# Two tiles counted in a row before the applying products of both, in the first phase of layer 1

## The reference

```python
# layer 0 (gated, with edge types)
src_h = h[src] @ W_msg.T + b_msg
emb = edge_embed[jnp.clip(edge_type, 0, NUM_EDGE_TYPES)]
msg = src_h + emb
messages = jax.ops.segment_sum(msg, dst, num_segments=num_nodes)
h_new = _gru_cell(messages, h[:num_nodes], W_ih, W_hh, b_ih, b_hh)
x = layernorm(x + h_new)
# layer 1 (attention-like weights)
proj = feat @ fc_weight.T
w = sigmoid(e(proj[src], proj[dst]) * gate(proj[src], proj[dst]))
rst = (1 + eps) * feat + segment_sum(feat[src] * w, dst) / deg
x = layernorm(x + rst)
```

## Time and profile before

| what | value |
|---|---|
| median of 3 runs | 3123.31 us (3120.69 to 3128.86) |
| the profiled execution, own time | 3125.21 us |
| its span, first to last instruction | 3121.9 us |
| mean granted TensorE clock over the span | 0.774 |
| busy over the span | DVE 87%, PE 66%, POOL 65%, ACT 53% |

### The profile page before, as it was taken

One profiled execution on the slowest core, in us unless ns is written; L12 is line 12 of the kernel. 1 busy time (PEld: TensorE's weight loads), 2 busy tenths in 40 slices (PEclk: granted clock), 3 DMA queues, 4 the chain that ended last, 5 costly groups with the idle time before them and its releaser, 6 DMA issues. The chain is left out here.

```text
span 3121.9 us, 64562 instructions
## 1 busy us (share of the span) xinstructions
PE 2069.9 (66%) x14172; PEld 1774.5 (57%) x14172; DVE 2721.6 (87%) x13432; ACT 1639.6 (53%) x3644; POOL 2034.8 (65%) x2108
## 2 busy tenths in 40 slices
PE   5899999999873555555555555555555555555555
PEld 4588888888543454544545544554545545454455
DVE  3499899899477899999989999999999999999995
ACT  1287777777334444554445454555445444454543
POOL 1057677777203677777777777777777777777760
PEclk9999999999997666676666777667666676667665
DMA  4233333333206444444444444444444444444441
GB/s 104 64 86 98 94 98 97 96 95 98 79 24 199 129 133 142 134 140 134 134 140 133 140 134 137 137 137 137 133 142 133 140 134 133 142 133 140 133 136 42
DMA packets 251978, 375.77 MB, mean 120 GB/s; under 512 B 107569, under 2 KB 168922, under 8 KB 251834
## 3 DMA queue, kind: packets, MB, share of 16 engines
q0 software_dynamic: 99600, 272.13, 30.1%
q1 hardware_dynamic: 150022, 101.31, 11.8%
q10 hardware_dynamic: 2212, 0.60, 0.1%
HBM read 350.21 MB, written 23.65 MB: 120 GB/s over the span
## 5 line engine op out<-in xcount | busy, mean ns | idle before, releaser
L1511 POOL DMA_INDIRECT got<-rows,idx x1624 | 1551.0, 955 | 546.0 <-issue 500.7
L1712 PE MATMUL sum_ps<-whot,got 128*128 128x128 f32 x3264 | 697.6, 384 | 525.7 <-DVE whot L1523 426.1
L1712 PEld LDWEIGHTS sum_ps<-whot,got 128*128 128x128 f32 x3264 | 602.2, 276 | 604.1 <-DVE whot L1523 477.4
L1705 PE MATMUL er_ps<-win,hot_t 128*128 128x128 bf16 x4932 | 508.3, 278 | 399.8 <-ACT hot_t L1653 365.8
L1705 PEld LDWEIGHTS er_ps<-win,hot_t 128*128 128x128 bf16 x4932 | 453.4, 130 | 448.2 <-ACT hot_t L1653 401.3
L788 POOL DMA_INDIRECT got<-y_rows,idx x448 | 460.0, 1027 | 198.2 <-issue 133.9
L1523 DVE TENSOR_SCALAR whot<-iota_f,dl,w_s 128x128 f32<-128x128 f32 x1632 | 455.6, 359 | 144.6 <-ACT w_s L1658 144.5
L947 ACT CAST cols<-c_ps 128x318 fp32r<-128x318 f32 x1176 | 493.1, 440 | 145.3 <-PE c_ps L1033 107.3
L979 PE MATMUL span_ps<-y_parts,cols 128*126 128x256 f32 x2968 | 568.5, 319 | 0.2 <-ACT cols L947 0.2
L1649 ACT ACTIVATE apart<-dst_b,less 128x512 bf16<-128x512 int16 x406 | 290.0, 714 | 326.2 <-DMA dst_b<-dst_row 320.4
L979 PEld LDWEIGHTS span_ps<-y_parts,cols 128*126 128x126 f32 x2968 | 453.4, 192 | 5.3 <-issue 1.0
(11 more groups left out here) (248 smaller groups left out, 2023.7 us busy)
## 6 DMA issues: line engine op xcount, KB each, us to landing
dst_b<-dst_row SPq DMA_DIRECT2D x59, 512.0 KB, 4.1
got<-rows,idx POOLq DMA_INDIRECT x1624
dst_b<-dst_row SPq DMA_DIRECT2D x59, 384.0 KB, 4.0
win<-parts SPq DMA_DIRECT2D x118, 96.0 KB, 3.7
got<-y_rows,idx POOLq DMA_INDIRECT x448
parts<-split SPq DMA_DIRECT2D x13, 384.0 KB, 7.0
y_rows<-y_parts SPq DMA_DIRECT2D x1, 3332.0 KB
rows<-nodes SPq DMA_DIRECT2D x13, 256.0 KB, 2.5
```

Of the source, the lines that this page charges most:

```text
L1511: pool.indirect_dma_start(got[:, c, i, :], None, rows, bass.IndirectOffsetOnAxis(ap=idx1[:, c, i:i + 1], axis=0)).then_inc(gathered[c], 16)
L1705: mm = pe.matmul(er_ps[:, c, i * D:(i + 1) * D], hot_t[:, c, i * P:(i + 1) * P], win[:, int(c >= HALF), part, :], start=(part == 0), stop= ...
L1712: mm = pe.matmul(sum_ps[:, 0:P], got[:, c, i, D:2 * D], whot[:, c, i, :], start=(c == 0 and i == 0), stop=(c == NS - 1 and i == STEP - 1))
```

## The change

The counts are issued two at a time. At an even t the loop issues the counts of tiles t and t + 1, each with its own waits. At an odd t it issues none. What follows at each t (applying products, `ready`, `post`, the products of the bodies) stays where it was. Tile 20 is counted alone. Number and shape of all instructions stay the same, and no other engine's program changes.

```diff
                             for t in range(CG):
-                                n, s = 2 * CG * k + CG * h + t, (CG * h + t) % RING
-                                pe.wait_ge(made, n + 1)
-                                if not first or CG * h + t >= CB:
-                                    pe.wait_ge(c_copied, n - CB + 1)
-                                pe.matmul(c_ps[:, (CG * h + t) % CB, 0:HW], left[:, s, :], right[:, s, :],
-                                          start=True, stop=True).then_inc(counted, 1)
+                                n = 2 * CG * k + CG * h + t
+                                if t % 2 == 0:
+                                    for u in range(t, min(t + 2, CG)):
+                                        m, s = n - t + u, (CG * h + u) % RING
+                                        pe.wait_ge(made, m + 1)
+                                        if not first or CG * h + u >= CB:
+                                            pe.wait_ge(c_copied, m - CB + 1)
+                                        pe.matmul(c_ps[:, (CG * h + u) % CB, 0:HW], left[:, s, :], right[:, s, :],
+                                                  start=True, stop=True).then_inc(counted, 1)
                                 if t >= BLOCKS and not (first and h == 0):
                                     if t == BLOCKS:
                                         ready(g - 1)
```

## The result

| | before | changed |
|---|---|---|
| median | 3125.11 us (4 runs, 3120.69 to 3128.86) | 3147.61 us (4 runs, 3144.41 to 3148.80) |
| span of the profiled execution | 3121.9 us | 3142.6 us |
| first to last count (the touched stage) | 649.9 us | 669.7 us |
| mean granted clock over the span | 0.774 | 0.758 |

The ratio is 1.0069, 95% interval 1.0054 to 1.0085: the changed kernel is slower by 22 us. 3141 was forecast, with a range of 3128 to 3149. Of the 20.7 us between the two spans, 19.8 lie between the first and the last count.

A forecast was written before the change was run, and what follows sets the result against it. TensorE was taken to bound the touched stage. Group beginnings +18.5, written-out part +1.2 and pairs -2.2 made +17.5 us: 3142.7 from the profiled 3125.2, which lay 1.9 above the median, so 3141 expected, range 3128 to 3149.

The forecast's parts named there:

- TensorE sets the pace, and the loss reaches the end: Touched stage: TensorE busy 589 of 600 us, waiting 10.8 us for VectorE; its gain or loss reaches the stage's end.
- Where a group begins, 0.41 us at nine of ten: Loop groups' beginnings: two products (0.24 us) and `ready` (0.17) come behind the wait for tile 0's copy; 18.5 us in all.
- free kind: Group beginnings, one of ten, where the count of tile 3 doesn't wait for a copy, as at group 23: loss 0.
- The written-out part, 0.3 us each: Four groups in the written-out part wait in the same way at their beginning: 0.3 us each, 1.2 us in all.
- Gain inside a group, 0.01 us a pair, of which half was taken: Pairs (4, 5) to (18, 19), 440 in all: gain between 0 and 4.4 us, taken as 2.2 us.
- No wait inside a group: A pair's second count does not wait for the copy or matrices: zero added, with 0.04 to 0.23 us to spare.
- The granted clock stays 0.99: Touched stage: the granted clock was expected still at 0.99 in the changed kernel's profile.
- That the loss is only two products a start (no change): Rival for group beginnings: `ready` is issued ahead, pairs gain the full 0.01 us; +0 to +9 us, some 3129; chance 0.19.
- That pairs give something large back: Rival, faster: each pair inside a group gives back 0.066 us, for 3114 us; chance 0.05.
- That every pair waits: Rival, much slower: pairs inside groups wait for copies, not only group beginnings; 15 us more, 3156; chance 0.13.

The follow-up runs named there:

- e5: Changed kernel, but ScalarE copies only 26 of 53 blocks of tile 0's counts in each group of the loop: 3137.6 us, ratio 1.0043 to the kernel before.
- e3: Changed kernel with `ready` issued ahead of the counts of tiles 2 and 3, not behind them: 3135.2 us, ratio 1.0035 to the kernel before.
- e2: Kernel before with only the count of tile 3 moved right behind that of tile 2, other counts single: 3148.1 us, ratio 1.0077 to before.
- e4: Changed kernel with the old order of counts in the group behind the loop's turn, one of ten: 3143.2 us, ratio 1.0058 to the kernel before.
- e1: Changed kernel with tiles 0 to 3 counted singly as before, pairs only from tile 4: 3123.5 us, ratio 0.9992 to the kernel before.

## Why the prediction was right

The sign held, and so did the mechanism by which most of the loss comes. The forecast was +17.5 us, measured are +22.5. Two errors of opposite sign are in it: a term for the clock is missing (4.7 us), and the pairs' gain is 2.9 too small. That the time still lies inside the range is in part luck, since no bound of the range had the clock in it. By its own steps:

- *TensorE sets the pace, and the loss reaches the end.* Right, save that the 10.8 us at the turns are no wait for VectorE (437.89 against 441.15, above). The part behind the last count took 2328.7, 2328.6 and 2332.6 us before, and 2332.9, 2335.1 and 2327.5 in the changed kernel: no difference beyond its spread.
- *Where a group begins, 0.41 us at nine of ten.* Right. The starts grew by 68.4 - 51.1 = 17.3 us over 45 groups. Five of these are of the free kind (group 23: 0.01 us), so it is 0.43 at the other 40. Each part was shown by itself: the wait for the copy of tile 0 by e5, `ready`'s share by e3 (0.20 at group 18, forecast 0.17), and that the step alone makes the loss by e2. At group 24 it was 0.56, forecast 0.55.
- *The written-out part, 0.3 us each.* Right: tile 2 to tile 4 took 0.30 us more in each of groups 2 to 5 (0.99 to 1.29 us).
- *Gain inside a group, 0.01 us a pair, of which half was taken.* Mis-sized. The rests gave back 4.2 us over 45 groups, 0.012 a pair, so about 5 over all, and not 2.2. The 0.01 from the rows was right, and halving it was not. The estimate by the Trainium skill, page "TensorE: Matmul & The Clock Gate", section "Back-to-back issue gap", would have given 6.6: nearer than my 2.2, though by too large a gain a pair, 15 ns against 12. The section itself calls its formula that of the isolated gap and says that a stream of matmuls with a weight load each departs from it. So it does here: two counts in a pair start 0.145 us apart at the median, not the 0.135 of the formula.
- *No wait inside a group.* Right: no count from tile 5 on waited for a copy in the changed kernel, and the rests got shorter. One group of ten (22) is an exception, its rest 0.04 longer and not 0.11 shorter, around two products at a body's end. It lies between tiles 16 and 18, 1.29 us before and 1.39 now. From the second of those two products to the second applying product behind it took 0.47 us with a count between them and takes 0.43 without, so the count that moved away had cost only 0.04 there.
- *The granted clock stays 0.99.* Wrong. It was 0.97, and this is the one step that failed. I had priced the groups behind a turn as all others, at 0.41. The four cost 71.2 - 65.9 = 5.3 us, and with all three profiles of each kernel (71.2, 72.1, 72.1 against 65.9, 65.4, 66.1) 6.0. Of that, 4 x 0.41 less 4 x 0.09 of the pairs, 1.3, had been counted. The rest, some 4.7 us, I put down to the longer stretches at 1.2 GHz. Group 6, which has the same order at its start and no pause in front, gives a check. Its tile 2 to tile 4 grew by 0.53 us (1.47 to 2.00), and its rest shrank by 0.14. From the first count to tile 20 the four groups behind a turn took 52.5 us in each profile before and 58.5, 59.0 and 59.8 in the changed kernel; less 4 x 0.39 this leaves 5.0 us for the clock. The stretches are 10.2 us long in each profile before, and 23.9, 27.3 and 27.3 changed. The old order in those groups took them back to 10.2 (e4).

Added up for the first profile: 17.3 in 45 starts, 1.5 in groups 0 to 6, 5.3 at the turns, -4.2 in 45 rests and -0.1 from tile 20 to tile 2: the 19.8 us of the stage.

The rivals: that the loss is only two products a start (no change) is out by the 0.25 us before the first applying product, and by e3. That pairs give something large back is out by e1. That every pair waits is out by the rests. What I missed was a fourth one: that a change just behind a pause can lengthen the stretch at the lower clock.

## What to carry to other kernels

A wait is not lost time while the engine has something else to issue behind it: read what runs in its shade before moving an instruction ahead of a wait, since everything that it passes comes out into the open, semaphore instructions included. When such a wait recurs at a fixed place, fill it with independent work from elsewhere in the period (here products that were due four tiles earlier, 6 us); and check what a batch of two gains per instruction first, for here it was 0.012 us.

## What the runs showed of the hardware

- At the loop's turn TensorE pauses for 2.3 to 3.0 us in both kernels (three profiles each), though the matrices and the copy that its next count needs are ready some 3 us before that count (2.9 to 3.5). In the same place its clock goes to 1.2 GHz for nothing, 3.4 or 6.8 us: 6.8 in none of 12 turns of the kernel before, and in 11 of 12 of the changed one. The length went with when the clock fell (never 6.8 us where it fell over 0.5 us behind the first count) and, where it fell within 0.5 us of it, with the order of the counts (11 of 13 against 0 of 6). The longer stretches cost about 1.2 us a turn, as much as three ordinary starts. The Trainium skill, page "TensorE: Matmul & The Clock Gate", section "HAM oscillation — how this bites in real kernels", describes pauses that bring the clock down again and again; the trace agrees in kind.
- Changing from bf16 counts to fp32 applying products costs next to nothing on TensorE: 360 changes fewer brought 4.2 us, 0.012 each.
- A count released by a copy starts 0.14 to 0.15 us after the copy's end, at the groups' beginnings of every kernel here. `ready` behind such a count put the next product 0.25 us after it; ahead of the counts, 0.02.
